# Banded attention: the residue order of a head pair is made on chip instead of being stored in DRAM twice

## The reference

```
OFFSETS = 0..32, 48, 64, 96, 128, 192, 256, 384
q, k, v = split(x @ Wqkv + bqkv)                 # 16 heads of 16
scores  = stack([sum(q * shift(k, d)) for d in OFFSETS]) * scale + pos_bias   # -inf where n < d
out     = sum_d softmax(scores)[d] * shift(v, d)
x = x + (out * sigmoid(x @ Wgate + bgate)) @ Wout + bout
```

## Time and profile before

| what | value |
|---|---|
| median of 3 runs | 3871.4 us (3869.67 to 3877.59) |
| the profiled execution's own time | 3860.39 us |
| its span | 3858.7 us |
| PE, DVE, ACT, POOL busy over the span | 78%, 44%, 35%, 13% |
| clearing of stack rows at the start (L674, DVE) | x3, 3472 ns each |

### The profile page before, as it was taken

One profiled execution on the slowest core, in us unless ns is written; L12 is line 12 of the kernel. 1 busy time (PEld: TensorE's weight loads), 2 busy tenths in 40 slices (PEclk: granted clock), 3 DMA queues, 4 the chain that ended last, 5 costly groups with the idle time before them and its releaser, 6 DMA issues. The chain is left out here.

```text
span 3858.7 us, 99901 instructions
## 1 busy us (share of the span) xinstructions
PE 2995.9 (78%) x45340; PEld 1721.1 (45%) x45340; DVE 1690.7 (44%) x2814; ACT 1363.9 (35%) x1358; POOL 494.7 (13%) x395
## 2 busy tenths in 40 slices
PE   0466767686767676768994899989999999997898
PEld 0244545454545454543452344444444444443345
DVE  5123333333333333344044666566566666574302
ACT  0414242433342423123001454445554555554300
POOL 0101020111010111000002121111122121210000
PEclk9678888887888797879976899999999999998896
DMA  5546465645554555422923232222222222212294
GB/s 128 133 84 140 101 148 106 143 103 127 107 141 96 142 103 140 83 98 79 422 115 77 44 70 55 51 50 51 55 59 54 51 59 51 59 34 91 106 421 176
DMA packets 232389, 419.65 MB, mean 109 GB/s; under 512 B 112922, under 2 KB 141412, under 8 KB 215588
## 3 DMA queue, kind: packets, MB, share of 16 engines
q1 hardware_dynamic: 206740, 360.34, 36.5%
q10 hardware_dynamic: 25232, 52.99, 4.5%
HBM read 316.49 MB, written 94.40 MB: 106 GB/s over the span
## 5 line engine op out<-in xcount | busy, mean ns | idle before, releaser
L1353 DVE TENSOR_REDUCE b_tops<-b_slot 128x8 f32<-128x1024 f32 x576 | 680.4, 1220 | 361.6 <-PE b_slot L1210 182.5
L1390 ACT ACTIVATE b_probs<-b_slot 128x1024 f32<-128x1024 f32 x576 | 582.9, 1023 | 550.8 <-PE b_slot L1210 394.9
L1230 PE MATMUL b_outT_ps<-b_probs,b_v 128*17 128x128 f32 (+3 forms) x4608 | 318.1, 384 | 6.2 <-ACT b_probs L1390 5.5
L738 DVE TENSOR_REDUCE a_tops<-a_slot 128x16 f32<-128x1024 f32 x128 | 156.4, 1222 | 362.4 <-PE a_slot L543 361.9
L1210 PE MATMUL b_slot<-b_q_stack,b_k_stack 99*128 99x512 bf16 (+3 forms) x1280 | 274.7, 321 | 43.5 <-DVE b_tops L1353 32.8
L1210 PE MATMUL b_slot<-b_k_stack,b_q_stack 96*128 96x512 bf16 (+3 forms) x1280 | 266.8, 323 | 29.0 <-DVE b_tops L1353 20.1
L780 ACT ACTIVATE a_probs<-a_probs 128x1024 f32<-128x1024 f32 x128 | 133.4, 1053 | 349.3 <-DVE a_probs L729 335.2
L563 PE MATMUL a_slot<-a_bias_q,a_ident 128*128 128x512 bf16 x256 | 96.8, 468 | 196.4 <-DMA a_k_stack<-orders_dram 176.4
L1157 POOL TENSOR_SCALAR_AFFINE_SELECT b_probs<-b_probs 128x1024 f32<-128x1024 f32 x128 | 139.8, 1093 | 809.7 <-ACT b_probs L1390 809.7
L599 PE MATMUL a_outT_ps<-a_probs,a_v_near 128*17 128x64 f32 (+1 forms) x8448 | 147.6, 232 | 87.0 <-issue 84.2
L813 ACT ACTIVATE a_parts<-a_parts 128x1024 bf16<-128x1024 bf16 x96 | 198.1, 2063 | 28.1 <-POOL a_parts L462 14.2
(11 more groups left out here) (217 smaller groups left out, 4328.2 us busy)
## 6 DMA issues: line engine op xcount, KB each, us to landing
f_w_ring<-in_L_ffn_w_dram SPq DMA_DIRECT2D x128, 1024.0 KB, 9.4
orders_dram<-a_parts ACTq DMA_DIRECT2D x96, 512.0 KB
a_k_stack<-orders_dram SPq DMA_DIRECT2D x128, 256.0 KB, 6.7
a_q_stack<-orders_dram SPq DMA_DIRECT2D x64, 384.0 KB, 4.6
parts_dram<-b_parts SPq DMA_DIRECT2D x96, 256.0 KB
a_q_stack<-orders_dram SPq DMA_DIRECT2D x64, 256.0 KB, 5.4
a_k_stack<-orders_dram SPq DMA_DIRECT2D x128, 128.0 KB, 7.6
b_k_stack<-parts_dram SPq DMA_DIRECT2D x64, 256.0 KB, 6.7
```

Of the source, the lines that this page charges most:

```text
L738: ins = dve.tensor_reduce(tops[:, h, :, :].rearrange("p k t -> p (k t)"), src[:, :].rearrange("p (t c) -> p t c", c=64), AX.X, ALU.max)
L1230: ins = pe.matmul(outT_ps[32 * h:32 * h + HD + 1, first:last], v1[b % 2][:, j, HG * g + h, :], src[:, base + first:base + last], start=u = ...
L1353: ins = dve.tensor_reduce(out, src, AX.X, ALU.max)
L1390: act.activation(probs_of(b, g, u, h)[:, :], slot_of(step)[:, :], ACT.Exp).then_inc(taken_act, 1)
```

## The change

The DRAM copy holds the tokens' order alone (`parts_near`), half the bytes. The stacks are split: `q_near` and `k_near` (token order, rings of four, loaded by DMA) and `q_far` and `k_far` (residue order, rings of three). A new step `turn` fills a pair's far stacks from its near ones, per head: ACT turns k, POOL turns q. The three `turn` steps of the division are gone, the DMA of a part follows the part at once, and `mrow` has 8 DMAs of half the size. A single shifted `perm` tile replaces eight.

```
-        return [(step, b, half, which) for step in ("part0", "rest1", "turn0", "part1", "part2", "turn1", "turn2")]
+        return [(step, b, half, which) for step in ("part0", "rest1", "part1", "part2", "store2")]
...
-            seq += [("vin", b, g), ("S", b, g, 0)] + place[0] + top[0] + [("S", b, g, 1)] + operands(n + 3) + place[1] + top[1]
-            seq += [("S", b, g, 2)] + place[2] + [("S", b, g, 3)] + ([] if late else operands(n + 4)) + top[2] + place[3] + top[3]
-            seq += ([("fparts",) + after] if more else []) + near + place[4] + ...
-            seq += far[0:4] + ([("mt",) + after, ("mrow",) + after] if more else []) + (operands(n + 4) if late else [])
+            seq += [("vin", b, g), ("S", b, g, 0)] + place[0] + top[0] + [("S", b, g, 1)] + operands(n + 4) + turned(n + 3) + place[1] + top[1]
+            seq += [("S", b, g, 2)] + place[2] + [("S", b, g, 3)] + top[2] + place[3] + top[3]
+            seq += ([("fparts",) + after] if more else []) + turned(n + 4) + near + place[4] + ...
+            seq += far[0:4] + ([("mt",) + after, ("mrow",) + after] if more else []) + operands(n + 5)
...
-            upto = 2 if waiting[0][0] in ("part0", "part1") else 1
+            upto = 2 if waiting[0][0] != "store2" else 1
...
+                    elif kind == "turn":      # GpSimd
+                        if two := last_use(b, g, pair, BY_RESIDUE):
+                            pool.wait_ge(filled, two)
+                        pool.wait_ge(stacked[near], STACK * count(f"stack{near}", "stack", b, g, pair))
+                        for h in range(2):
+                            pool.tensor_copy(q_far[far][0:QK_ROWS, h, :].rearrange("p (r a) -> p r a", r=LINKS),
+                                             q_near[near][0:QK_ROWS, h, :].rearrange("p (a r) -> p r a", r=LINKS)).then_inc(turned_q, 1)
...
-                            sp.wait_ge(spilled[part], 16 * count(f"turn{part}", f"turn{part}", b, g // 2, "k"))
-                        if 2 * (b * G + g) + pair >= 3:
+                            sp.wait_ge(spilled[part], 16 * count("store2", "store2", b, g // 2, "k"))
+                        if two := last_use(b, g, pair, BY_TOKEN):
...
+                            for order, rows in enumerate((q_near[ring(b, g, h // 2, BY_TOKEN)], q_far[ring(b, g, h // 2, BY_RESIDUE)])):
+                                sp.dma_start(rows[QK_ROWS:ALL_ROWS, h % 2, :], neg_rows[PARTS * h:PARTS * (h + 1), order, :]).then_inc(mrows_in, 16)
...
-                        if h % 2 == 0:
-                            pe.wait_ge(stacked[n], STACK * count(f"stack{n}", "stack", b, g, h // 2))
+                        turns = 2 * count("turn", "turn", b, g, h // 2) - 1 + h % 2
+                        pe.wait_ge(turned_q, turns)
+                        pe.wait_ge(turned_k, turns)
...
+                    elif kind == "turn":      # ScalarE, same waits
+                        for h in range(2):
+                            act.activation(k_far[far][0:QK_ROWS, h, :].rearrange("p (r a) -> p r a", r=LINKS),
+                                           k_near[near][0:QK_ROWS, h, :].rearrange("p (a r) -> p r a", r=LINKS), ACT.Copy).then_inc(turned_k, 1)
...
-    scratch["orders"] = nc.dram_tensor("orders_dram", [2, 2, 2, 8, PARTS, HD, 2, N], BF16)
+    scratch["parts_near"] = nc.dram_tensor("parts_near_dram", [2, 2, 2, 8, PARTS, HD, N], BF16)
```

More of the change, by code:

```diff
@@ L218, in band_schedule, with ring @@
     return out + waiting
-def ring(b, g, pair):
-    return (2 * (b * G + g) + pair) % 3
+def ring(b, g, pair, depth):
+    return (2 * (b * G + g) + pair) % depth
 def pair_of(n):
@@ L241, in band_attention @@
         if step[0] == "stack":
-            name = f"stack{ring(*step[1:])}"
+            name = f"stack{ring(*step[1:], BY_TOKEN)}"
             total[name] = nth[name, step] = total.get(name, 0) + 1
```

130 lines of the change are left out of this document (70 added, 60 removed).

## The result

| | before | after |
|---|---|---|
| median of the runs | 3874.5 us (3869.7 to 3895.7, 4 runs) | 3748.5 us (3745.1 to 3754.9, 4 runs) |
| profiled execution | 3860.4 us, span 3858.7 | 3749.7 us, span 3747.8 |
| mean granted clock | 0.887 | 0.896 |
| first scores of the first batch / of the last group | 186.9 / 1648.8 us | 182.6 / 1541.3 us |

The changed kernel is faster: its time is 0.9667 of the other's, 95% interval 0.9628 to 0.9705. The forecast was 3801 us and the range ended at 3751, so the sign was right and the size was not: 126 us between the medians in place of 70, and 111 us between the two profiled executions. Of these 111 us, 107.5 have been won when the first scores of the last group start, all of it inside the banded stage.

A forecast was written before the change was run, and what follows sets the result against it. PE was taken to be bound by maxima products waiting for the stack's DMA (176.4 us); terms -60 + 3 + 0 + 15 - 13 - 5 + 0 - 10 = -70 us from 3871.4 gave 3801 us, range 3751 to 3862.

The forecast's parts named there:

- The reading of the bound: Banded stage: PE's largest wait is maxima products waiting for the stack's DMA, 176.4 us in 31 places.
- the new last waits: Before mx2 in first and fourth groups, PE waits for ACT's or POOL's turn instead, 80 to 100 us together.
- the first group: Its 5.73 us wait before mx2 stays and only changes its name: +0.4 x 8 = +3 us.
- T: Time of POOL's strided turn copy of one head: 2.0 us taken, lower bound 1.04, upper bound 4.2.
- The step that failed: Middle batches: second and third groups have a long filler between S1 and mx2, so hardly wait for the stack's DMA.
- the second group: Only batch 0's was counted: its waits of 6.74 us before mx0 and 6.10 before mx2 go, -13 us.
- The fetch term: Long gaps ending at `issue` beside transfers: half the traffic gives some back, -10 us, from -30 to +10.
- The prologue: Start of the kernel: three early turns, v's copy at its old time, more clearing; 0 us, from -5 to +5.
- `mrow` at +15: Four more DMA issues of 0.71 us each delay the maximum's rows before S0: +15 us, between 0 and 18.6.
- The third group: Last batch: the 4.78 us wait before mx2 goes, -5 us; middle batches 0, from -1.5 to +3 each.
- The fourth group: mx2 starts 8.5 us earlier, 12.8 us after S0 in place of 21.3; seven batches, -60 us (-45 to -80).
- The rival in which all of the wait goes: Whole kernel: the 176 us stack wait and the slow restart behind large gaps vanish, 3670 us; chance 0.03.

The follow-up runs named there:

- e8: Kernel before, both orders still spilled to DRAM but only the tokens' order loaded (far output differs): 3743.9 us, ratio 0.9673.
- e1: Changed kernel with the old DMA bytes put back by 512 KB DRAM copies ahead of each pair's q and k loads: 3767.3 us, ratio 0.9725.
- e2: Kernel before with only the tokens' order spilled and loaded, half the bytes (far output differs): 3703.0 us, ratio 0.9578.
- e7: Changed kernel without the turn, residue products reading the tokens' order (far output differs): 3628.5 us, ratio 0.9366.
- e10: Changed kernel with the turn ahead of the division, mrow in four DMAs and the first three turns moved in the prologue: 3648.2 us, ratio 0.9429.
- e3: Changed kernel with the maximum's rows (mrow) written by four DMAs per group in place of eight: 3724.7 us, ratio 0.9619.
- e5: Kernel before with the maximum's rows (mrow) written by eight DMAs per group, two per head in place of one: 3922.8 us, ratio 1.0142.

## Why the prediction missed

**Right.** The reading of the bound, and the new last waits. mx2 of the fourth group came 12.5 us after S0, 12.8 forecast; the first group changed the name of its wait and kept its length (5.73 to 5.53 us); T was 2.04 us, 2.0 forecast; a pair's load landed in 2.9 us (3.8 assumed); the issue of half a row transfer costs as much as that of a whole (0.64 to 0.74 us against 0.71). Eight of them run from 1014.61 to 1020.53 us, 5.9 us, 5.7 forecast. The rule of the Trainium skill that was cited for it (DMA: Bandwidth & Descriptors, Bandwidth: transfers under 64 KB are dominated by their descriptors) is about how long a transfer takes, not about its issue. The equal issues fit it and do not test it. The waits for the turn are 58.5 us where 80 to 100 were named: they come to 4.6 us a batch in the first group and 4.2 in the fourth, and three of fifteen are missing.

**The step that failed** is the sentence that the second and third groups of a middle batch "hardly wait for this DMA". For the second group that is true of the stack's entry, 0.6 us a batch, and it was taken for the whole effect of the transfer. The group won 39 us, not 13, though the rows of the maxima took back about 1 us a batch at its end. Two parts of the gain were outside the sum: the load of 4 KB rows that landed in its value products and lengthened the gaps at `issue` there (8.4 to 5.7 us a batch), and mx2, 1.7 us earlier. e8 shows that they belong to the size of the loads: with it alone halved the group falls to 36.4 us. In e1, which has the changed kernel's order and all the traffic of before, the group stays at 38.0 us, so traffic as such does not lengthen it. The fetch term (-10) was put as one number over the stage and measured 20 us in the two entries; the ten long gaps were counted, but not in which groups they lie. In the first batch, too, the second group won 15.9 us, more than the two waits of 12.8 that were counted.

**Mis-sized terms.** The first group was to lose 3 us and won 6.1, of which 4.3 in the first batch. The prologue was put at 0 and won 4.3: halved loads and spills win 13.7 us there (e2), and the three turns give most of it back (e7 and e10 start 13.5 and 15.3 us before after). `mrow` at +15 was too little: 24 us by e3. The third group looks right (-3 for -5), and that is luck: with its share of `mrow` it was to lose some 7 to 9 us, and shorter gaps at `issue` (7.8 to 6.4 us a batch) hide the loss.

**The fourth group.** -54.5 us for -60. The size is near, and two errors hide in it. The group was read from the fifth batch, whose distance from S0 to mx2 (21.3 us) is the shortest of the middle six, 22.5 in the mean; and the S0 that ends it, the next batch's first, now waits 0.9 us for the rows in the mean, which was put at 0.2.

**The comparison.** The profiled execution of before was 11 us under the median then known and 14 under the one measured with the changed kernel; that of after is 1 us over its own. So 15 of the 56 us by which the gain was larger than forecast are no mechanism of the change, and 41 are terms of the sum.

**What the runs say of the sum as a whole.** It was built from waits in place, each with its next one. That gave the right new waits, but it hid that two large effects of opposite sign were being netted: half the bytes are worth 167 us by themselves (e2), the turn costs 120 (e7), the split rows 24 to 52 (e3, e5), the ring with its early loads is worth 94 to 134. The forecast of 70 was the difference of numbers of which three are larger than itself. The rival in which all of the wait goes gave 3670. The change as it stands is 79 us above it, and e10 reaches 22 us below it with three more edits.

What stays open: why the gaps at `issue` lengthen beside a transfer (e1 and e8 show that they do, not through which resource), and how the 15 us between the profiled execution of before and its median come about. A smaller question was not tried either: whether the far rows of `mrow` could be issued from another queue.

## What to carry to other kernels

Before a change that trades bytes for copies is timed as a whole, time its halves: what half the bytes alone are worth, and what the copy alone costs. A copy that is put on an engine with an in-order queue must stand behind its data in time (one more buffer) and ahead of work that nobody awaits (here the spills of the division). Where several small transfers stand ahead of a load on one issuing queue, each costs 0.7 us and can cost it twice: to who waits for it, and to who waits for the load.

## What the runs showed of the hardware

- Issue of a transfer from SP: 0.64 to 0.74 us for three partitions of 2 KB (6 KB in all), the same as for 12 KB.
- A copy of 96x1024 bf16 with a step of 32 bytes on the read side: 1.27 us on VectorE, 2.04 on GpSimd, 2.06 on ScalarE. GpSimd and ScalarE differ by 1%.
- PE's gaps at `issue`, about 1.5 to 2 us each 128 matmuls of the value products, sum to 171.5 us in e2 and 177.3 in e1. With those at other lines it is 187 us at a DMA share of 0.31 and 237 at 0.42. A load of 4 KB rows that landed beside them made one of 4.57 us, its halved form one of 1.37. They are the largest repeated idle time that is left in e10: 93.0 and 72.0 us in the waits of PE.
- The two bias matmuls ahead of a maxima product take 0.60 us at a granted clock of 1.00 and 1.01 to 1.03 us at 0.50: the two clock levels, seen in one group of after (1022.52 and 1034.26 us).
